# ScalarE sums the FFN weights' magnitudes; their rounding and the output weights' split move into attention's first turns

## The reference

```
xn = layernorm(h) * gamma + beta
q, k, v = split(xn @ w_qkv)
out = softmax(q k^T / 8) v        (within an image of 36 tokens)
h = h + out @ w_out + b_out
```

```
def weight_quant(w):
    scale = 1.0 / max(mean(abs(w)), 1e-5)
    return clip(round(w * scale), -1, 1) / scale
```

## Time and profile before

| | |
|---|---|
| median of 3 runs | 276.17 us (273.78 to 276.98) |
| profiled execution | 276.51 us |
| its span | 274.7 us |
| PE busy | 232.7 us (85%) |
| DVE busy | 191.8 us (70%) |
| ACT busy | 154.6 us (56%) |
| POOL busy | 115.9 us (42%) |
| mean granted TensorE clock | 0.929 |

### The profile page before, as it was taken

The page is one execution under the profiler, slowest core; times in us unless marked ns, Lnnn a source line. Parts: engine busy times, 40 slices in busy tenths (PEclk is TensorE's granted clock), DMA queues, the critical chain, the costliest instruction groups (busy, mean ns, idle before and its releaser), DMA issues.

```text
span 274.7 us, 6271 instructions
## 1 busy us (share of the span) xinstructions
PE 232.7 (85%) x2392; PEld 182.4 (66%) x2392; DVE 191.8 (70%) x520; ACT 154.6 (56%) x296; POOL 115.9 (42%) x139
## 2 busy tenths in 40 slices
PE   1955999798596967988898999998999986999992
PEld 1732566577585965444496785975578965999982
DVE  1767999568999589779759789298882516344465
ACT  3629668245579754677589668292722454445510
POOL 9121494011212878464660005206108878655400
PEclk9995799779779799999999998999998998899998
DMA  6998372332800079940043006940813994722252
GB/s 201 335 258 189 93 257 50 68 69 68 243 31 4 2 122 198 201 87 2 2 43 45 0 2 67 138 56 0 119 34 58 144 165 59 106 23 26 26 143 64
DMA packets 23362, 26.09 MB, mean 95 GB/s; under 512 B 10842, under 2 KB 19091, under 8 KB 23109
## 3 DMA queue, kind: packets, MB, share of 16 engines
q0 software_dynamic: 5888, 11.24, 28.4%
q1 hardware_dynamic: 17445, 14.45, 18.5%
HBM read 30.46 MB, written 4.66 MB: 128 GB/s over the span
## 4 chain that ended last, share of the span: by engine, by line
PE 46%; DVE 24%; ACT 9%; issue 7%; another core or an unknown queue 2%; POOL 1%; DVEq 0%; ACTq 0%
PE bank L882 11%; PE bank L634 6%; PE bank L549 5%; PE bank L894 4%; DVE arena_k L1016 3%; PE bank L565 2%; PE bank L724 2%; PE bank L606 2%; PE bank L701 2%; PE bank L742 2%; PE bank L594 2%; DVE st L947 2%; DVE arena L1023 1%; PE bank L579 1%
## 5 line engine op out<-in xcount | busy, mean ns | idle before, releaser
L634 PE MATMUL bank<-tri,idh 128*128 128x512 f16 x148 | 40.1, 394 | 0.0
L1381 DVE TENSOR_TENSOR arena<-bank,arena 128x360 f32<-128x360 f32 x16 | 8.5, 533 | 25.9 <-PE bank L882 15.6
L1795 POOL TENSOR_TENSOR arena<-arena,ri 128x432 f32<-128x432 f32 x8 | 7.5, 941 | 39.0 <-DVE ri L1065 39.0
L1864 POOL DMA_INDIRECT y_sum<-arena x12 | 17.9, 1492 | 12.7 <-ACT arena L1734 10.3
L634 PEld LDWEIGHTS bank<-tri,idh 128*128 128x128 f16 x148 | 14.1, 101 | 10.9 <-issue 2.2
L1771 POOL TENSOR_TENSOR rs<-arg,mhalf 128x1 f32<-128x1 f32 (+1 forms) x20 | 11.9, 594 | 22.2 <-DVE arg L951 20.7
L1873 POOL DMA_INDIRECT arena<-x_scratch,arena x14 | 14.5, 1038 | 15.9 <-DVE arena L1429 11.9
L882 PE MATMUL bank<-arena,arena_v 96*128 96x180 f16 x192 | 18.9, 267 | 2.6 <-DVE arena L1368 2.6
L565 PE MATMUL bank<-arena,arena_k 96*128 96x288 f16 (+2 forms) x144 | 21.0, 312 | 0.0
L882 PEld LDWEIGHTS bank<-arena,arena_v 96*128 96x128 f16 x192 | 18.2, 109 | 3.4 <-DVE arena L1368 3.3
L1722 ACT ACTIVATE arena<-bank 128x360 f32<-128x360 f32 x16 | 7.5, 470 | 20.7 <-PE bank L882 15.7
(11 more groups left out here) (285 smaller groups left out, 628.5 us busy)
## 6 DMA issues: line engine op xcount, KB each, us to landing
arena_k<-in_w POOLq DMA_DIRECT2D x8, 384.0 KB, 5.8
arena_v<-in_w POOLq DMA_DIRECT2D x8, 384.0 KB, 8.3
arena_v<-in_xT SPq DMA_DIRECT2D x6, 288.0 KB, 4.0
arena_v<-in_wqkv SPq DMA_DIRECT2D x3, 576.0 KB, 11.4
arena_v<-v_scratch SPq DMA_DIRECT2D x32, 54.0 KB
v_scratch<-arena SPq DMA_DIRECT2D x4, 384.0 KB, 2.7
arena_k<-in_w POOLq DMA_DIRECT2D x8, 192.0 KB, 7.1
arena_v<-in_w POOLq DMA_DIRECT2D x8, 192.0 KB, 9.2
```

What stands on the lines that cost most here:

```text
L634: mm(bank[IDLE][:, :], idh[:, :], tri[:, 0:1].broadcast_to([128, 512]), start=True, stop=True)
L1864: nc.gpsimd.indirect_dma_start(y_sum[k][:, :], bass.IndirectOffsetOnAxis(ap=sum_at[:, k, e:e + 1], axis=0), ys[:, e, D * k:D * k + D], Non ...
```

## The change

Five things are done together.

- DVE's two reductions of the weights' magnitudes go. ACT does them instead with `Abs` and an accumulated sum (`accum_out`), behind `kq_high` of the first half and ahead of the attention loop; the elementwise result goes into a throwaway area `wide` in the arena that held v, so ACT first waits for v's stores.
- PE's two `wmean` matmuls move from ahead of the keys and queries into turn 0, between its two `keys_queries`. DVE's four small steps move likewise into turn 0, between its two `kq_low`.
- DVE's clip and round move from turns 3, 4 and 5 into turns 1 and 2. ACT's `w2q` moves from turn 6 to turn 2, `wiq` from behind the loop to turn 3.
- The output weights' high half moves from ACT's turn 5 to turn 1, with its wait for the load; the low half from DVE's turn 7 to turn 2.
- `woraw` now lies in the arena that held v. So SP's wait for the last queries ahead of the `woT` load goes. The load keeps its place behind the 32 `Vbd` loads. POOL's wait for wo_lo ahead of expert 4's load goes too.

```diff
+        wide = arena[:, KC * T + HP * D:KC * T + HP * D + 2048]
-        woraw = arenaK[:, K_W:K_W + HP * D].rearrange("p (k n) -> p k n", k=HP)
+        woraw = arena[:, KC * T:KC * T + HP * D].rearrange("p (k n) -> p k n", k=HP)
...
-        plan("wmean")
         for hp in range(HP):
             plan("k", hp, 0)
...
                 for hp in (2 * s, 2 * s + 1):
                     plan("k", hp, 1)
                     plan("q", hp, 1)
+                    if hp == 0:
+                        plan("wmean")
...
                 wait_full(pool, "S", PAIRS - 1)
-                pool.wait_ge(wo_lo, 1)
...
-            wait_full(sp, "q", HP - 1, 1)
             load(woraw, "woT")
...
-            bk = claim(pe, "wmean")
...
+            def weight_sums():
+                bk = claim(pe, "wmean")
+                pe.wait_ge(wq_part, 2)
...
                 if s < 3:
-                    for hp in (2 * s, 2 * s + 1):
-                        keys_queries(hp, 1)
+                    keys_queries(2 * s, 1)
+                    if s == 0:
+                        weight_sums()
+                    keys_queries(2 * s + 1, 1)
...
-            v.tensor_reduce(wsum[0:HF, 0:1], stage13[:, :, :], AX.XY, ALU.add, apply_absolute_value=True).then_inc(wq_part, 1)
-            v.tensor_reduce(wsum[:, 1:2], stage2[:, :, :], AX.XY, ALU.add, apply_absolute_value=True).then_inc(wq_part, 1)
...
-            bk = wait_full(dve, "wmean")
...
+            def weight_means():
+                bk = wait_full(dve, "wmean")
...
+                if s == 1:
+                    st_.then(v.tensor_scalar(stage2[:], stage2[:], sw[:, 1:2], 1.0, ALU.mult, ALU.min))
+                    v.tensor_scalar(stage2[:], stage2[:], -1.0, MAGIC, ALU.max, ALU.add).then_inc(wq_sum, 1)
+                if s == 2:
+                    st_.settle()
+                    v.tensor_scalar(stage13[:], stage13[:], -1.0, MAGIC, ALU.max, ALU.add).then_inc(wq_sum, 1)
                 if s < 3:
-                    for hp in (2 * s, 2 * s + 1):
-                        kq_low(hp, 1)
+                    kq_low(2 * s, 1)
+                if s == 0:
+                    weight_means()
+                if s == 1:
+                    st_.do(v.tensor_scalar(stage13[:], stage13[:], sw[0:HF, 0:1], 1.0, ALU.mult, ALU.min))
+                if s == 2:
+                    dve.wait_ge(wo_hi, 1)
+                    v.tensor_tensor(woT[:, 1], woraw, woT[:, 0], ALU.subtract).then_inc(wo_lo, 1)
+                if s < 3:
+                    kq_low(2 * s + 1, 1)
...
-                if s == 3:
-                    st_.then(v.tensor_scalar(stage2[:], stage2[:], sw[:, 1:2], 1.0, ALU.mult, ALU.min))
-                    v.tensor_scalar(stage2[:], stage2[:], -1.0, MAGIC, ALU.max, ALU.add).then_inc(wq_sum, 1)
-                if s == 4:
-                    st_.then(v.tensor_scalar(stage13[:], stage13[:], sw[0:HF, 0:1], 1.0, ALU.mult, ALU.min))
-                if s == 5:
-                    v.tensor_scalar(stage13[:], stage13[:], -1.0, MAGIC, ALU.max, ALU.add).then_inc(wq_sum, 1)
-                if s == PAIRS - 1:
-                    dve.wait_ge(wo_hi, 1)
-                    v.tensor_tensor(woT[:, 1], woraw, woT[:, 0], ALU.subtract).then_inc(wo_lo, 1)
...
             for hp in range(HP):
                 kq_high(hp, 0)
+            act.wait_ge(loaded("w_in"), 16)
+            act.wait_ge(loaded("w_out2"), 16)
+            act.wait_ge(v_stored, 16 * NT)
+            for w, n in ((stage_a[0:HF, :], 0), (stage2[:, :, :].rearrange("p m n -> p (m n)"), 1)):
+                r, m = w.shape
+                st_.do(a(wide[0:r, 0:m], w, ACT.Abs, accum_out=wsum[0:r, n:n + 1]))
+                st_.settle()
+            act.sem_inc(wq_part, 2)
...
                 if s < 3:
                     for hp in (2 * s, 2 * s + 1):
                         kq_high(hp, 1)
-                if s == 5:
+                if s == 1:
                     act.wait_ge(loaded("woT"), 16)
                     a(woT[:, 0], woraw, ACT.Copy).then_inc(wo_hi, 1)
+                if s == 2:
+                    act.wait_ge(wq_sum, 1)
+                    a(w2q[:], stage2[:], ACT.Identity, bias=nmagic[:, 0:1]).then_inc(wq_done, 1)
+                if s == 3:
+                    act.wait_ge(wq_sum, 2)
+                    a(wiq[:], stage13[:], ACT.Identity, bias=nmagic[0:HF, 0:1]).then_inc(wq_done, 1)
...
-                if s == 6:
-                    act.wait_ge(wq_sum, 1)
-                    a(w2q[:], stage2[:], ACT.Identity, bias=nmagic[:, 0:1]).then_inc(wq_done, 1)
-            act.wait_ge(wq_sum, 2)
-            a(wiq[:], stage13[:], ACT.Identity, bias=nmagic[0:HF, 0:1]).then_inc(wq_done, 1)
             table(ACT.Silu)
```

More of the change, by code:

```diff
@@ L551, in _ @@
                     fills(ins, "v", i, c)
-            bk = claim(pe, "wmean")
[L553 to L557, removed]
+            def weight_sums():
+                bk = claim(pe, "wmean")
+                pe.wait_ge(wq_part, 2)
+                pe.wait_ge(zeroed, 1)
+                mm(bk[:, 0:1], ones[0:HF, :].broadcast_to([HF, 128]), wsum[0:HF, 0:1], start=True, stop=True)
+                ins = mm(bk[:, 1:2], ones[:, :].broadcast_to([128, 128]), wsum[:, 1:2], start=True, stop=True)
+                fills(ins, "wmean")
             def keys_queries(hp, n):
@@ L988, in _ @@
                 v.tensor_tensor(wqkv[:, 1, :, o], wqkvraw[:, :, o], wqkv[:, 0, :, o], ALU.subtract).then_inc(wqk_lo, 1)
-            dve.wait_ge(loaded("w_in"), 16)
-            dve.wait_ge(loaded("w_out2"), 16)
-            v.tensor_reduce(wsum[0:HF, 0:1], stage13[:, :, :], AX.XY, ALU.add, apply_absolute_value=True).then_inc(wq_part, 1)
-            v.tensor_reduce(wsum[:, 1:2], stage2[:, :, :], AX.XY, ALU.add, apply_absolute_value=True).then_inc(wq_part, 1)
             for i in range(NT):
@@ L1056, in _ @@
             dve.wait_ge(hbias, 1)
+            def weight_means():
+                bk = wait_full(dve, "wmean")
+                st_.do(v.tensor_scalar(mw[:, 0:1], bk[:, 0:1], 1.0 / (2 * FH * D), 1e-5, ALU.mult, ALU.max))
+                frees(v.tensor_scalar(mw[:, 1:2], bk[:, 1:2], 1.0 / (FH * D), 1e-5, ALU.mult, ALU.max), "wmean")
+                st_.settle()
+                wait_evac(dve, "wmean")
+                st_.do(v.reciprocal(sw[:], mw[:]))
+                st_.then(v.tensor_scalar(mwd[:], mw[:], 1.0 / 127.0, None, ALU.mult))
             for s in range(PAIRS + 4):
```

## The result

The changed kernel takes 288.29 us (median of 4 runs, 285.66 to 289.31) against 276.58 us for the kernel before in the same set; the ratio is 1.0444, 95% interval 1.0326 to 1.0563. It is slower by about 11.7 us, inside the predicted 283.5 to 290 us and 1 us above the predicted 287.3. Medians are of all runs, while a ratio leaves out runs of a slower kind (here those more than 1.5% above the fastest of the same kernel), so the two can differ a little.

A forecast was written before the change was run, and what follows sets the result against it. It took ACT's wait for the output weights' load, behind SP's 32 issues, then the loop through ACT and PE, as bounds; 11.35 - 0.3 = +11.05 us on 276.51 gave 287.5, median 287.3, range 283.5 to 290 us.

The forecast's parts named there:

- The wait that moves: ACT, end of turn 1: stands some 11 to 12 us for the output weights' load, issued behind SP's 32 loads.
- The landing: Output weights' load, issued at 69.18 us behind SP's 32 issues, still lands 4.8 us later, at 73.98 us.
- the sum: Whole kernel: 11.35 - 0.3 = +11.05 us on the profiled 276.51 us gives 287.5 us; 287.3 us for the median.
- From the landing to pair 3's exponential: ACT and DVE steps after the landing at 73.98 us: exponential starts at 83.2 against 71.85 us, 11.35 us later.
- Turns 3 to 7: DVE loses 4.8 us, but ACT's and PE's loop sets the pace; only 0.3 us to be had.
- Turn 0 and what is ahead of it: Turn 1 starts 0.6 us earlier, ACT's sums cost 3.3 us in idle; worth nothing in the sum, hidden by ACT's wait.
- the bounds: Turn 0 and ahead: -3 us (TensorE's half-clock stretch shortened) to +3 us (sums twice as long), neither reaching the end.
- second rival: Load issued or landed before ACT asks, so no wait; turns 1 and 2 cost +1.9 us, 278.1 us; chance 0.02.
- the third: Load in time and turns 3 to 7 set by DVE: -4.8 against +2.2 us, 273.5 us; chance 0.02.
- first rival: Wait as deep, but DVE sets the later turns and 4.8 us leave it: 283.1 us; chance 0.11.

The follow-up runs named there:

- Experiment 1: Changed kernel with the output weights' load issued ahead of SP's 32 loads of v instead of behind them; 278.13 us, ratio 1.0048 to the kernel before.
- experiment 3: Kernel before with the output weights' part alone (copy in v's arena, SP's wait gone, halves in turns 1 and 2); 288.37 us, ratio 1.0403.
- experiments 4: Changed kernel with the output weights' load issued behind 24 of SP's 32 loads of v; 281.39 us, ratio 1.0137 to the kernel before.
- experiment 5: Changed kernel with the output weights' load issued behind 16 of SP's 32 loads of v; 272.37 us, ratio 1.0071 to the kernel before.
- experiment 6: Kernel before with the sums' part alone (ACT's Abs sums, wmean matmuls and means' steps in turn 0); 270.43 us, ratio 0.996.
- experiment 8: Kernel before with the sums' part plus DVE's state-weight preparation moved from turn 9 to the end of turn 8; 270.35 us, ratio 1.0012.
- experiments 1 to 6: Includes one not named singly, the second: changed kernel, output weights' halves back in ACT turn 5 and DVE turn 7; 277.74 us, ratio 1.0024.
- experiment 7: Kernel before with the clipping and rounding alone moved (DVE turns 1 and 2, ACT turns 2 and 3); 272.58 us, ratio 1.0049.

## Why the prediction was right

**The wait that moves.** Right in place, cause and size: 11.70 us of idle, where "11 to 12" were forecast, ended by the load's landing. Experiment 1 removes it by the load's place alone, experiment 3 makes it by the output weights' part alone, and experiments 4 and 5 show that it is paid by issues ahead of the load, up to the point where the load lands before ACT asks. Each of the 32 starts, 0.83 us, is short beside the 4.1 to 4.8 us of the load; their sum is not.

**The landing.** Forecast 73.98 us; the copy began at 72.16. SP began its loads 0.7 us earlier in this execution, issued them in 26.46 instead of 27.17 us, and the load took 4.4 instead of 4.8 us. These three are the 1.8 us by which the profiled execution (285.66) stayed under the 287.5 of the sum. They vary from profile to profile: the first of the 32 was issued between 41.27 us and (experiment 3) 43.24 us. The prediction had this start set by the end of POOL's clearing, and unmoved. In the changed kernel the clearing ended at 40.24 us, and SP then waited 1.0 us more for v's stores to land; in experiment 3 that wait was 2.1 us. How much of the 0.7 us is the change's own was not tested. The forecast of the median was 1.0 us low and the sum for the profiled execution 1.8 us high; that the median came so near is in part luck.

**From the landing to pair 3's exponential.** Forecast 83.2 - 73.98 = 9.2 us, measured 81.32 - 72.16 = 9.16. The order on DVE was as worked out, step by step:

```profile
73.81 0.61 DVE L1078 TENSOR_TENSOR arena<-arena 128x432 f16<-128x432 f32 x1 [9.03 <-ACT arena L1554]
74.34 1.22 DVE L1084 TENSOR_SCALAR stage_a<-stage_a 96x2048 f32<-96x2048 f32 x1
75.47 0.92 DVE L1006 TENSOR_TENSOR arena_k<-bank,arena_k 64x288 f16<-64x288 f32 x2
...
76.77 1.35 DVE L1093 TENSOR_TENSOR arena<-arena 128x1152 f16<-128x1152 f32 x1
78.03 0.92 DVE L1006 TENSOR_TENSOR arena_k<-bank,arena_k 64x288 f16<-64x288 f32 x2
...
80.68 0.61 DVE L1071 TENSOR_TENSOR arena<-bank,mx 128x432 f32<-128x432 f32 x1
```

**Turns 3 to 7.** Forecast 15.3 us from pair 0's values to pair 4's, measured 98.05 - 82.67 = 15.38, against 15.57 before. DVE, rid of 4.8 us, waits instead: it has idle times of 0.47 us before each sum from turn 6 on. Three rounds of the loop took 10.77 us, 3.6 each. So 4.8 us taken off an engine that was busy without a gap gave 0.2 us.

**Turn 0 and what is ahead of it.** The gain was mis-sized: pair 1's exponential came at 57.66 us against 59.93, 2.27 us earlier, of which the first keys had about half already (37.22 against 38.30). The rest has a part that I held to the bounds, TensorE's clock: granted 1.00 in turn 0 after, 0.50 before. ACT's sums took 2.96 us, where 3.3 were estimated, and left 1.10 us of idle ahead of the first exponential; no table load came in with `Abs`. As forecast, none of turn 0's gain reached the end: ACT was done with turn 1 2.2 us earlier (60.5 against 62.63 us) and waited all the longer.

**The rivals.** The second and third need a load that is in time; experiment 1 makes that case and measures it: 1.0048, or 1.3 us slower, where the second rival had 1.9 and the third a gain. The first rival needed 13 us or less from pair 0's to pair 4's values.

The parts, each put alone into the kernel before, are 1.0403 (output weights), 1.0049 (rounding) and 0.996 (sums). Multiplied they make 1.041, inside the interval of the whole change's 1.0444 (1.0326 to 1.0563).

## What to carry to other kernels

When a step moves forward, move its wait with it in your mind: ask when what it waits for can be there, and for a load that is what stands ahead of it in its issuer's list, each issue at its own price, not the transfer's bytes. Taking an old wait out of that list does nothing if the load keeps its place. And an engine that is busy without a gap is not for that reason the path: look for the loop through the others before you pay to relieve it.

## What the runs showed of the hardware

**The same idle, two clocks.** Ahead of pair 0's scores PE was idle for 1.85 us in the changed kernel and in experiment 6. TensorE was then granted full clock (2.4 GHz) in the first, half (1.2 GHz) in the second. The stretches, as start:end, length, busy by engine, granted clock, DMA share and GB/s; the changed kernel's:

```profile
49.70:51.40 1.70, 1.70 (x17) 1.49 (x17) 1.22 (x2) 0.60 (x3) 0.00 (x0) 1.00 0.39 86
```

and that of experiment 6:

```profile
52.00:54.00 2.00, 2.00 (x12) 1.58 (x11) 1.10 (x3) 1.13 (x4) 0.00 (x0) 0.50 0.27 62
```

Experiment 8 has the same code as experiment 6 as far as turn 8, had the same idle, and ran on at full clock (on another chip; experiment 5, on the same chip as 6, did so too):

```profile
51.05 1.57 PE L568 MATMUL bank<-arena,arena_k 96*128 96x288 f16 x12
```

Of the eight profiles with an idle of 1.85 us here (the changed kernel, experiments 1 to 6 and 8), seven went on at full clock. Experiment 3, which leaves everything ahead of turn 0 as before, is one of them, where the profile of before had 2.39 us and half. From pair 0's exponential to pair 1's it took 7.60 us in experiment 6 and 6.54 in experiment 8, 7.16 in the kernel before and 5.96 in experiment 3. A clock that is worth 1.1 to 1.2 us here is thus no property of the kernel alone, and a single profile doesn't show what it costs on the mean. What else decides it was not tried.

**DVE is held up while POOL works.** In the kernel before, DVE's last small step of the means (128x2 numbers) took 2.10 us:

```profile
39.51 2.10 DVE L1010 TENSOR_SCALAR mwd<-mw 128x2 f32<-128x2 f32 x1
```

It ended at 41.61 us, and POOL's clearing at 41.59 us. In experiment 3 the clearing ended at 40.84 us, the step began at 40.78 and took 0.15 us:

```profile
40.78 0.15 DVE L1009 TENSOR_SCALAR mwd<-mw 128x2 f32<-128x2 f32 x1
```

In experiment 7 the clearing ended later, at 43.03 us, and the step was held until then:

```profile
40.69 2.37 DVE L1010 TENSOR_SCALAR mwd<-mw 128x2 f32<-128x2 f32 x1
```

PE's idle ahead of turn 0 follows: 1.85 us in experiment 3, 2.39 in the kernel before, 3.29 in experiment 7. It hangs on whether POOL's clearing still runs when DVE comes to that step. Experiment 8 shows DVE held up likewise on a tensor_tensor of 96x32 numbers (1.12 us, against 0.18 in the kernel before) and on a copy (1.73 against 0.25). The Trainium skill, "SBUF — State Buffer", section on who interferes with whom, has that VectorE and GpSimd share a pair of SBUF ports as an exclusive lock, which tensor_scalar and copies can take, and for which a tensor_tensor with both inputs in SBUF contends with GpSimd's reads; these rows agree, and the page would have spoken against experiment 8's place.
